# Attention and MXFP4 FFN on one core: two of eight key tiles of the value product in rounded high and low parts

## The reference

```
xn  = layernorm(x)                               # x: (4, 1024, 256)
qkv = xn @ w_qkv.T                               # 16 heads of 128; q and k rotated (RoPE)
att = softmax(q @ k.T / sqrt(128)) @ v @ w_out.T
ffn = gelu(xn @ mx(up) + up_bias) @ mx(down) + down_bias    # mx(): MXFP4 blocks of 32, dequantised
out = x + att + ffn
```

## Time and profile before

| | us |
|---|---|
| median of 3 runs | 2511.87 (2510.96 to 2513.03) |
| the profiled execution, its own time | 2514.25 |
| its span, first to last instruction | 2512.4 |
| busy: PE, PEld, DVE, ACT, POOL | 2457.9, 2133.9, 2023.0, 1351.9, 1841.8 |

### The profile page before, as it was taken

How to read it: one execution, slowest core, us unless ns; L and a number is a source line. 1 busy time by engine, 2 the same in 40 slices (tenths; PEclk the granted TensorE clock), 3 DMA queues, 4 the chain that set the end, 5 groups by cost and what they waited for, 6 DMA issues and landing times. The chain is left out here.

```text
span 2512.4 us, 41984 instructions
## 1 busy us (share of the span) xinstructions
PE 2457.9 (98%) x12656; PEld 2133.9 (85%) x12656; DVE 2023.0 (81%) x3204; ACT 1351.9 (54%) x2518; POOL 1841.8 (73%) x1485
## 2 busy tenths in 40 slices
PE   6999999999999999999999999999999999999899
PEld 5788888888888888888888888888888888888788
DVE  7778878787887878788787878878787887878677
ACT  6455555554555555555556555555555555555333
POOL 7678777777877777787777778777777877787131
PEclk9999999999999999999999999999999999999999
DMA  4455555556655555556655555556565555555742
GB/s 120 125 135 131 140 134 142 134 145 159 163 140 135 141 134 145 135 130 169 163 146 135 145 136 130 140 133 167 146 168 138 130 140 133 140 127 126 230 143 68
DMA packets 233876, 354.30 MB, mean 141 GB/s; under 512 B 37856, under 2 KB 95584, under 8 KB 233696
## 3 DMA queue, kind: packets, MB, share of 16 engines
q1 hardware_dynamic: 233824, 353.72, 54.3%
HBM read 66.26 MB, written 18.87 MB: 34 GB/s over the span
## 5 line engine op out<-in xcount | busy, mean ns | idle before, releaser
L921 PE MATMUL o_ps<-keys_first,v_rows 128*128 128x256 f32 x4096 | 928.5, 380 | 7.9 <-DMA keys_first<-turned_blocks 7.9
L595 ACT ACTIVATE probs<-s_ps,neg_max 128x1024 f32<-128x1024 f32 x512 | 571.4, 1116 | 676.6 <-DVE neg_max L693 671.9
L921 PEld LDWEIGHTS o_ps<-keys_first,v_rows 128*128 128x128 f32 x4096 | 764.4, 190 | 108.6 <-DMA keys_first<-turned_blocks 9.6
L921 PE MATMUL s_ps<-seq_parts 128*128 128x512 f32 x3072 | 835.9, 408 | 20.7 <-ACT probs L595 11.1
L693 DVE TENSOR_REDUCE neg_max<-s_ps 128x1 f32<-128x1024 f32 x512 | 610.8, 1203 | 165.2 <-PE s_ps L921 165.1
L921 PEld LDWEIGHTS s_ps<-seq_parts 128*128 128x128 f32 x3072 | 576.5, 189 | 145.1 <-ACT probs L595 18.4
L705 DVE STREAM_TRANSPOSE turned_blocks<-probs 128x512 f32<-128x512 f32 x1024 | 663.1, 685 | 18.5 <-DVE mx_q L779 3.7
L471 POOL TENSOR_TENSOR rope_a<-rope_a,cos 128x512 f32<-128x512 f32 x253 | 328.7, 1299 | 452.2 <-ACT rope_b L587 452.0
L921 PE MATMUL slot_ps<-seq_parts,w_parts 128*128 128x512 f32 x1506 | 388.1, 393 | 4.6 <-DMA seq_parts<-xnt_parts 4.5
L476 POOL TENSOR_TENSOR rope_a<-rope_a,rope_b 128x512 f32<-128x512 f32 x253 | 326.7, 1291 | 19.9
L474 POOL TENSOR_TENSOR seq_parts<-rope_a,rope_b 128x512 fp32r<-128x512 f32 x253 | 326.5, 1291 | 19.9
(11 more groups left out here) (108 smaller groups left out, 2137.3 us busy)
## 6 DMA issues: line engine op xcount, KB each, us to landing
keys_first<-turned_blocks SPq DMA_DIRECT2D x2048, 128.0 KB, 2.7
w_raw<-in_w_qkv SPq DMA_DIRECT2D x96, 256.0 KB, 3.2
seq_parts<-xnt_parts SPq DMA_DIRECT2D x14, 1024.0 KB, 7.9
wo_raw<-in_w_out SPq DMA_DIRECT2D x64, 128.0 KB, 2.5
y<-in_x SPq DMA_DIRECT2D x16, 256.0 KB, 3.2
ln_x<-in_x SPq DMA_DIRECT2D x16, 256.0 KB, 3.4
xnt_parts<-ln_hi SPq DMA_DIRECT2D x16, 256.0 KB, 2.8
xnt_parts<-ln_lo SPq DMA_DIRECT2D x16, 256.0 KB, 3.1
```

The costliest lines, as they stand in the source:

```text
L595: nc.scalar.activation(probs[:, k2 % 4, :], s_ps[k2 % 2][:, :], ACT.Exp, bias=neg_max[:, col:col + 1], accum_out=row_sum[:, col:col + 1]). ...
L921: ins = nc.tensor.matmul(out, w, m, start=(n == 0), stop=(n == len(terms) - 1))
```

## The change

Four edits, made together:

1. **The value product.** Key tiles 0 and 1 of each chunk (`SPLIT = 2`) are no longer fp32 matmuls. v is kept for them as v_hi (ScalarE) and v_lo (VectorE, `v_low`), the probabilities as p_hi (`probs_high`, a ScalarE copy of 128x512 from `keys_first`) and p_lo (`probs_low`, a GpSimd difference in place), and there are three fp32r matmuls a tile. The chain has two waits inside it.
2. **Rotations in two steps.** From the seventh group on, GpSimd does the two products and one sum (`rotated_sum`), ScalarE rounds it to qk_hi (`rotated_high`), GpSimd takes the difference (`rotated_low`). Their places in the step lists are written out, and `probs_low` stands between them.
3. **Fewer weight splits.** In the first sequence the split weights are stored to DRAM (`store_part`, `store_wo`); in the other three they are loaded back as hi and lo (`reload_part`, `reload_wo`), with no work on ScalarE and GpSimd.
4. `V_TILES` changes the order in which the token tiles of v are projected, so that the split ones come third.

```diff
             def values(i, k, first):
...
-                chain(o_ps[:, 0:CHUNK],
-                      [(v_rows[:, parity, kt, cols], keys_first[:, slot, :, kt, :]) for kt in range(BT)], o_ready)
+                out = o_ps[:, 0:CHUNK]
+                for kt in range(SPLIT, BT):
+                    nc.tensor.matmul(out, v_rows[:, parity, kt - SPLIT, cols], keys_first[:, slot, :, kt, :].bitcast(F32),
+                                     start=(kt == SPLIT), stop=False)
+                pe.wait_ge(p_hi_ready, c + 1)
+                for kt in range(SPLIT):
+                    nc.tensor.matmul(out, v_hi[:, parity, kt, cols], p_hi[:, slot, :, kt, :], start=False, stop=False)
+                    nc.tensor.matmul(out, v_lo[:, parity, kt, cols], p_hi[:, slot, :, kt, :], start=False, stop=False)
+                pe.wait_ge(p_lo_pool, c + 1)
+                for kt in range(SPLIT):
+                    last = nc.tensor.matmul(out, v_hi[:, parity, kt, cols], keys_first[:, slot, :, kt, :],
+                                            start=False, stop=(kt == SPLIT - 1))
+                last.then_inc(o_ready, 1)
```

GpSimd's new step (the five-instruction `rotate` calls are gone from it; `guess` and the weight splits stay ahead of this):

```diff
+                if k8 == 1:
+                    rotated_sum(p, "qk1", 2)
+                    if not first:
+                        rotated_low(p, "qk1", 1)
+                if k8 == 5 and more_pairs:
+                    rotated_sum(p + 1, "qk0", 2)
+                    rotated_low(p + 1, "qk0", 1)
+                if not (first and k == 0):
+                    probs_low(c - 1, (k - 1) % 2)
+                if k8 == 0 and not first:
+                    rotated_low(p, "qk1", 0)
+                    rotated_sum(p, "qk1", 1)
+                if k8 == 1:
+                    rotated_low(p, "qk1", 2)
+                    rotated_sum(p, "qk1", 3)
+                if k8 == 2:
+                    rotated_low(p, "qk1", 3)
...
```

("qk1", 0 to 3 are the groups 4 to 7.) ScalarE's new step:

```diff
+                if k % 8 == 5 and more_pairs:
+                    rotated_high(p + 1, "qk0", 1)
+                if k % 8 == 1 and not tail and not (first and k == 1):
+                    rotated_high(p, "qk1", 1)
...
+                    if k % 8 == 4 and more_pairs:
+                        rotated_high(p + 1, "qk0", 0)
+                    if k % 8 == 6 and more_pairs:
+                        rotated_high(p + 1, "qk0", 3)
+                    if k % 8 == 0 and not (first and k == 0):
+                        rotated_high(p, "qk1", 0)
+                    if k % 8 == 2:
+                        rotated_high(p, "qk1", 3)
+                    if not (first and k == 0):
+                        probs_high(i, k - 1)
                     if not (last and k == 15):
                         exponentials(t + 2, 2 * k + 2, first and k == 0)
+                    if k % 8 == 5 and more_pairs:
+                        rotated_high(p + 1, "qk0", 2)
+                    if k % 8 == 1:
+                        rotated_high(p, "qk1", 2)
                     g = group_at(k, 0, last)
```

with `rotated_high` waiting for the sum, `probs_high` for the moved keys, and `probs_low` for p_hi:

```diff
+            def probs_high(i, k):
+
+                act.wait_ge(keys_moved[k % 4], chunk_moves(i, k))
+                nc.scalar.activation(p_hi[:, k % 2], keys_first[:, k % 2, :, 0:SPLIT, :].bitcast(F32),
+                                     ACT.Copy).then_inc(p_hi_ready, 1)
...
+            def probs_low(c, slot):
+
+                pool.wait_ge(p_hi_ready, c + 1)
+                low = keys_first[:, slot, :, POOL_TILES, :]
+                nc.gpsimd.tensor_tensor(low, low.bitcast(F32), p_hi[:, slot, :, POOL_TILES, :].bitcast(F32),
+                                        ALU.subtract).then_inc(p_lo_pool, 1)
```

SP's queue, after the key moves of a chunk:

```diff
+                    for at, part in ((0, "qk0"), (2, "v"), (4, "qk1")):
+                        if k8 == at and PAIRS_PER_SEQ <= p + 1 < PAIRS:
+                            reload_part(p + 1, part)
+                        if k8 == at + 2 and p + 1 < PAIRS_PER_SEQ:
+                            store_part(p + 1, part)
+                            if p + 2 < PAIRS_PER_SEQ:
+                                load_part(p + 2, p + 2, part)
```

More of the change, by code:

```diff
@@ L45 @@
 MX_HALF = MX_COLS // 2
+SPLIT = 2
 def layer(nc, d):
@@ L512, in _, with step @@
                 rotate(pool, nc.gpsimd, 0, "qk1", n, "pool", n + 2).then_inc(qk_ready, 1)
-            def step(i, k, first, last):
+            def step(i, k, first, last, splitting):
+                c = i * 16 + k
                 if k >= 16:
+                    if k == 16:
+                        probs_low(c - 1, (k - 1) % 2)
                     return
                 k8 = k % 8
-                more = not (last and k >= 8)
                 p = i * 2 + k // 8
+                more_pairs = not (last and k >= 8)
+                more = splitting and not (isinstance(p, int) and p + 1 >= PAIRS_PER_SEQ)
                 if k8 == 0 and more:
@@ L523, in step @@
                     w_low(p + 1, "v")
-                if k8 == 3:
+                if k8 == 3 and splitting:
                     wo_low(p, 1)
@@ L669, in step @@
                         exponentials(t + 3, 2 * k + 3, first and k == 0)
-            steps(act, step)
+            steps_splitting(act, step)
             def gelu(g, f, first):
@@ L839, in _ @@
             row_max(1, 1)
+            for (place, part, n), bank in zip(FIRST_GROUPS, FIRST_BANKS):
+                if part == "v" and n in V_SPLIT:
+                    v_low(0, 0, n, bank)
             def step(i, k, first, last):
@@ L851, in step @@
                     turn(i, k, 1, first)
+                g = None if tail or (first and k == 0) else group_at(k - 1, 1, last)
+                if g and g[1] == "v" and g[2] in V_SPLIT:
+                    v_low(i * 2 + g[3], g[3] % 2, g[2], slot_ps[:, 1])
                 if (k - 1, 1) == LN_SLOT:
```

192 lines of the change are left out of this document (148 added, 44 removed).

## The result

The change took 2529.3 us (median of 4 runs, 2527.4 to 2533.4), and the kernel before beside it 2511.85 us: ratio 1.0067 [1.0055, 1.008]. It is **slower by 0.67%**; the forecast was 2527.0 us. The profiled execution spans 2527.5 us, 15.1 more than before; the medians are 17.4 us apart, because the profiled execution of the kernel before was 2.4 us above its median.

A forecast was written before the change was run, and what follows sets the result against it. TensorE, busy 98% of the span, was taken as the bound as long as nobody comes later. −36.9 + 15.0 + 33.6 + 1.6 + 1.8 = +15.1 us on 2511.9 gave 2527.0 us; range 2488 to 2545.

The forecast's parts named there:

- The matmuls: TensorE's value chain: 6 fp32r matmuls replace 4 fp32 ones, saving 0.144 us for each of 256 chunks, −36.9 us.
- Work that is hidden: ScalarE gains about 1 us in a 9.1 us step, VectorE's v_low costs zero, reloads add nothing: no time lost.
- GpSimd's longer train: Before the second head's scores (steps 3, 11): rotation 7 ends later, costing +15.0 us in even pairs, +33.6 in odd ones.
- The even pair's count: GpSimd's instructions from step 0 to the scores of step 3: a new TensorE wait of 1.0 us in 15 rounds, +15.0.
- The rival of a shorter train: Wait before the second head's scores: GpSimd's train is shorter than counted, 2496 us or down to 2475; chance 0.13.
- the other rivals: GpSimd leaves VectorE alone in step 8: 2495, chance 0.10; p_lo or keys late: 2543, 0.10; clock falls: 2565, 0.05.
- the clock rival: Odd pairs: if a 2.75 us wait lowers TensorE's clock, each loses 2.4 us or more, +38, 2565 us; chance 0.05.
- The odd pair: Step 8 to the second head's scores: TensorE stands 2.75 us instead of 0.65, 2.1 more in 16 rounds, +33.6.
- Round 0 and the ends: GpSimd's extra work in the first round, +1.6 us, and before p_lo in three first-sequence rounds, +1.8; ends 0.

The follow-up runs named there:

- matmuls_alone: Changed kernel without making p_hi and p_lo per chunk; same matmuls read a buffer filled once, two key tiles left out of the result: 2477.22 us, ratio 0.9853 to before.
- values_fp32: Changed kernel with edits 2 and 3 alone, value product all fp32, no p_hi, p_lo or v_low: 2513.74 us, ratio 0.9996 to the kernel before.
- phi_first: Changed kernel with ScalarE making p_hi before qk_hi(7) in steps 2 and 10: 2513.62 us, ratio 1.0001 to the kernel before.
- one_more: Changed kernel plus one spare GpSimd subtraction in steps 1 and 9, ahead of rotation 7's sum: 2574.09 us, ratio 1.0244 to the kernel before.
- low7_first: Changed kernel with GpSimd taking rotation 7's difference before p_lo in steps 2 and 10: 2526.05 us, ratio 1.0048 to the kernel before.
- combined_k9: Changed kernel reordered: p_hi, ln_lo, group 4's difference earlier, the layer norm's guess later, rotation 6 rounded before step 9's exponentials: 2475.80 us, ratio 0.9848 to before.
- values_fp32_filled: values_fp32 plus one spare GpSimd subtraction in step 5, where its trace shows a gap: 2538.02 us, ratio 1.0095 to the kernel before.

## Why the prediction was right

**The matmuls: right.** −36.9 predicted; the quiet steps give −41 (0.16 us a step, not 0.144), and matmuls_alone is 36 us below before.

**Work that is hidden: right for ScalarE's load, not for its order, and wrong for VectorE (below).** values_fp32 shows edits 2 and 3 at zero. ScalarE has the time for p_hi, but its place is not hidden: ahead of qk_hi(7) instead of behind, it is worth 17 us (phi_first).

**GpSimd's longer train: right.** The even pair's count was off by 0.1 us at low(7), and steps 2 and 3 lost 17.3 us against 16.8 predicted. TensorE itself stands only 0.73 us of the 1.0 us a pair. one_more (+1.0 and +1.2 us for one instruction) and low7_first (the wait moves to p_lo) show that it is the train as a whole. The rival of a shorter train falls with them. Of the other rivals none came in the change: VectorE's three quantising instructions there still take 4.24 us beside GpSimd (4.30 before), no value chain waits for p_lo in mid-run beyond 5.0 us in all, and the granted clock is 1.00 from 150 to 2340 us. A wait as long as the clock rival asks for came in combined_k9: in step 11 of round 7 TensorE stands 2.70 us, the granted clock falls to 0.50, and six scores take 2.42 us; after 2.39 and 2.55 us in rounds 3 and 11 it stays at 1.00.

**The odd pair: right in place, too large.** 31.5 against 23.3 us in 15 rounds. In an ordinary round it lost 1.8 us, not 2.1. I had one wait of 2.75 us; there were two, 1.33 + 0.74 = 2.07. The train ended 0.4 us sooner after step 8's start than counted, for rotation 7 was taken 17.48 us after it and not 17.82. The other 3.5 us of the difference are in step 11 of rounds 3, 7 and 11, which got shorter by 1.5, 1.2 and 0.9 us: there TensorE waited for the next sequence's xn, 4.5 us in all before and 1.5 after. That a TensorE which comes later finds more of it loaded is the likely reason; it was not tried. The sum has no such term.

**What was missed: ln_lo in step 6, +12.9 us.** The failing step is "Work that is hidden", which has VectorE gain nothing but v_low, "zero, at most 1 us", and asks only for its load. I looked for a change of VectorE's speed beside GpSimd in step 8 alone. A GpSimd instruction that is already running makes the small instructions of step 5 long as well: L973 takes 1.20 us in every round, where L789 slipped into a pause in 15 of 16 rounds before. ln_lo had only some 0.4 us of slack (1.2 us late, 0.84 us paid). Taking p_hi and p_lo out (matmuls_alone) removes the wait, and closing GpSimd's gap in a kernel that has neither (values_fp32_filled) brings it about. The Trainium skill (SBUF — State Buffer, section "Who interferes with whom") says that a tensor_scalar in a mode that uses two ports contends with GpSimd, and that the one that issues second is fully blocked. The traces agree, as far as they show it: the stretched instructions (L966 of values_fp32, L965, L967 and L969 of the filled kernel) are tensor_scalar and began second, L789 of the kernel before began first and was not stretched, and the reciprocal, which is no tensor_scalar, was not. In which mode they ran no trace says. The traces show besides that a tensor_scalar that starts during a GpSimd instruction is recorded as busy until that ends.

**Round 0 and the ends: wrong, small.** Instead of +3.7 us round 0 lost 0.6. Its waits were spread over other steps; why was not tried. In the last steps TensorE waited 4.70 us for keys, and the tail was shorter by about as much.

## What to carry to other kernels

When a helper engine has capacity but an output is late, count its train from the first instruction that had to wait to the last that is waited for, and look at the order on every engine that feeds it: five changes of order were worth 2.2% here, with no instruction removed. When an engine's load falls but its gaps close, look at small instructions of its neighbour: they may have lived in the gaps, even in gaps of less than 0.1 us. Separate a change's gain (matmuls_alone) from its cost early, for it shows what an ordering can win back.

## What the runs showed of the hardware

- A VectorE tensor_scalar of 128x8 took 0.16 to 0.17 us when it began while GpSimd stood still, even 0.01 us before GpSimd's next instruction (974.88 in the kernel before). When it began 0.07 to 0.12 us after the start of a GpSimd instruction of 1.26 to 1.31 us it took 1.19 to 1.23 us and ended with that, to 0.03 us. At a distance of 0.01 to 0.02 us both occur: 1.28 us (L966 of values_fp32) and 0.16 us (L965 of the filled kernel, rounds 3 and 15).
- A VectorE reciprocal of the same size took 0.20 us, begun 0.10 us into a GpSimd instruction (974.88 in values_fp32).
- The granted clock fell to 0.50 after TensorE had been busy 0.74 of 2.00 us (one_more, round 12), in 4 of the 12 even pairs with the same two waits (rounds 4 to 15), and in none of the three with a longer first wait (1.22 to 1.23 us, rounds 1 to 3). In rounds 1 to 15 of the kernel after and of the kernel before, none of the pairs shows this.
- After single waits of 2.39, 2.70 and 2.55 us (combined_k9, step 11 of rounds 3, 7 and 11) the clock fell once, after the one of 2.70.
